# Expert-attention scores: two 128-row products with doubled keys in place of three 64-row products per head

## The reference, cut to what matters

```python
q = _rope(jnp.einsum('bsd,hdp->bhsp', x, Wq))      # P = 64
k = _rope(jnp.einsum('bsd,hdp->bhsp', x, Wk))
v = jnp.einsum('bsd,bhse,hedp->bhsp', x, gv, Wv)
att = jax.nn.softmax(jnp.einsum('bhsp,bhtp->bhst', q, k) / np.sqrt(P), axis=-1)
o = jnp.einsum('bhst,bhtp->bhsp', att, v)
return jnp.einsum('bhsp,bhse,hepd->bsd', o, go, Wo)
```

## Time and profile before

| | |
|---|---|
| median of three runs | 3404.74 us (3403.65 to 3405.85) |
| span of the profiled execution | 3401.4 us |
| time around that span | not listed for that execution; the runs' median is 3.3 us above its span |
| TensorE matmul busy | 3233.1 us, 95% |
| VectorE, ScalarE, GpSimd busy | 2439.7 us (72%), 1961.5 us (58%), 1441.9 us (42%) |
| DMA | 295.18 MB, 32.9% of the 16 engines' span |
| granted TensorE clock | 0.995 of full speed |

### The profile page before, as it was taken

The page is one execution under the profiler, slowest core; times in us unless marked ns, Lnnn a source line. Parts: engine busy times, 40 slices in busy tenths (PEclk is TensorE's granted clock), DMA queues, the critical chain, the costliest instruction groups (busy, mean ns, idle before and its releaser), DMA issues.

```text
span 3401.4 us, 64468 instructions
## 1 busy us (share of the span) xinstructions
PE 3233.1 (95%) x18240; PEld 2378.9 (70%) x18240; DVE 2439.7 (72%) x4708; ACT 1961.5 (58%) x4509; POOL 1441.9 (42%) x1215
## 2 busy tenths in 40 slices
PE   1699999999999999999999999999999999997998
PEld 1577777777777777777777777777777777775765
DVE  6577777777777777777777777777777777775554
ACT  2466666656666666666666666666666666664121
POOL 4144355445443454345543554434534543442212
PEclk9999999999999999999999999999999999999999
DMA  5223333334233333233233332333332433333221
GB/s 165 76 71 87 95 90 85 77 76 109 76 84 87 84 98 81 75 100 96 69 87 76 96 98 77 76 104 81 84 87 68 114 81 75 84 75 110 72 83 62
DMA packets 115937, 295.18 MB, mean 87 GB/s; under 512 B 33856, under 2 KB 54592, under 8 KB 99264
## 3 DMA queue, kind: packets, MB, share of 16 engines
q1 hardware_dynamic: 115904, 294.78, 32.9%
HBM read 262.74 MB, written 31.98 MB: 87 GB/s over the span
## 4 chain that ended last, share of the span: by engine, by line
PE 85%; issue 6%; DVE 5%; ACT 3%; DMA 1%; POOL 0%; ACTq 0%; SPq 0%; DVEq 0%; POOLq 0%
PE bank L673 27%; PE bank L799 22%; PE bank L718 9%; PE bank L773 7%; PE bank L688 5%; PE bank L905 4%; PE bank L897 3%; PE bank L693 3%; PE bank L745 2%; PE bank L754 2%; ACT probs L957 2%; DVE uf L1239 1%; DVE oo L1232 1%; PE bank L694 1%; ACT pt_e L977 1%
## 5 line engine op out<-in xcount | busy, mean ns | idle before, releaser
L573 POOL TENSOR_TENSOR u_l<-uf,u_h 128x512 fp32r<-128x512 f32 x512 | 716.1, 1409 | 722.6 <-ACT u_h L1041 722.4
L1136 DVE TENSOR_REDUCE nmax<-bank 128x1 f32<-128x512 f32 (+3 forms) x1024 | 551.8, 579 | 305.0 <-PE bank L688 297.8
L673 PE MATMUL bank<-wv_h,xx 128*128 128x512 f32 x2048 | 755.0, 410 | 7.1 <-DVE vm L1157 7.1
L957 ACT ACTIVATE probs<-bank,nmax 128x512 f32<-128x512 f32 (+3 forms) x1024 | 590.7, 610 | 253.2 <-DVE nmax L1136 253.1
L1041 ACT ACTIVATE u_h<-uf 128x512 fp32r<-128x512 f32 x512 | 321.7, 632 | 696.9 <-DVE uf L1239 683.6
L673 PEld LDWEIGHTS bank<-wv_h,xx 128*128 128x128 f32 x2048 | 386.0, 188 | 155.8 <-issue 59.6
L718 PEld LDWEIGHTS bank<-ident_sb,probs 128*128 128x128 f32 x3328 | 388.3, 141 | 106.4 <-issue 51.3
L718 PE MATMUL bank<-ident_sb,probs 128*128 128x128 f32 x3328 | 451.3, 274 | 1.6 <-ACT stackT L1032 0.9
L569 POOL TENSOR_TENSOR v_sb<-v_next,zero_hb 128x512 f32<-128x512 f32 x64 | 74.2, 1160 | 891.9 <-PE bank L773 877.4
L799 PE MATMUL bank<-u_h,wo_h 128*128 128x512 f32 x1024 | 427.1, 417 | 5.0 <-ACT u_h L1041 3.2
L1239 DVE TENSOR_TENSOR uf<-oo,go 128x512 f32<-128x512 f32 x512 | 416.2, 823 | 8.8 <-POOL u_l L573 6.6
(11 more groups left out here) (141 smaller groups left out, 5164.2 us busy)
## 6 DMA issues: line engine op xcount, KB each, us to landing
go<-go_d SPq DMA_DIRECT2D x256, 512.0 KB, 6.5
xx<-xs_d SPq DMA_DIRECT2D x128, 512.0 KB, 3.5
oo<-scale_d SPq DMA_DIRECT2D x128, 128.0 KB, 2.9
a_d<-a_out SPq DMA_DIRECT2D x128, 128.0 KB, 2.3
pt_c<-in_x SPq DMA_DIRECT2D x16, 512.0 KB, 4.7
st<-in_wv SPq DMA_DIRECT2D x16, 512.0 KB, 5.8
st<-in_wo SPq DMA_DIRECT2D x16, 512.0 KB, 7.2
go_d<-go_turned SPq DMA_DIRECT2D x256, 8.0 KB
```

The costliest lines, as they stand in the source:

```text
L573: nc.gpsimd.tensor_tensor(u_l[:, e % 2], uf[:, e % 2], u_h.bitcast(f32)[:, e % 2], ALU.subtract).then_inc(ul_done, 1)
L673: last = nc.tensor.matmul(out, lhs, rhs, start=n == 1, stop=n == 3 * len(chunks))
L957: nc.scalar.activation(probs[:, s % 2, j, 0:w], sbank[j][:, 0:w], ACT.Exp, bias=nmax[:, 2 * s + j:2 * s + j + 1], **kw).then_inc(exp_done, 1)
L1136: nc.vector.tensor_reduce(nmax[:, 2 * s + j:2 * s + j + 1], sbank[j][:, 0:w], AX.X, ALU.max, negate=True).then_inc(nmax_ready, 1)
```

## The change

The query's high and low parts of one head are stacked on the 128 partitions: head 0 has its high part on partitions 0 to 63 and its low part on 64 to 127, head 1 the other way round (`q_hl`). The keys' high parts are held twice, on both halves (`k_hh`), and so are the low parts (`k_ll`). One matmul on 128 rows then gives high·high + low·high, a second one high·low + low·low. ScalarE and VectorE write one half each time, so every `QH` and `QL` becomes two instructions on 64 partitions. The second copy of the keys is made by four DMAs from one half of the tile to the other, issued by SyncE in `both_halves`; the scores wait for all four.

```diff
-        q_h = sb("q_h", [NP, S], f32r)
-        q_l = sb("q_l", [NP, S], f32r)
-        k_h = sb("k_h", [NP, S], f32r)
-        k_l = sb("k_l", [NP, S], f32r)
+        q_hl = sb("q_hl", [NP, 2, S], f32r)
+        k_hh = sb("k_hh", [NP, 2, S], f32r)
+        k_ll = sb("k_ll", [NP, 2, S], f32r)
...
+            def both_halves(n):
+
+                for i, (k, made, count) in enumerate(((k_hh, qk_high, 2 * n + 2), (k_ll, k_low, n + 1))):
+                    sp.wait_ge(made, count)
+                    for j in range(2):
+                        here, there = slice(j * P, (j + 1) * P), slice((1 - j) * P, (2 - j) * P)
+                        sp.dma_start(k.bitcast(f32)[there, j, :], k.bitcast(f32)[here, j, :]).then_inc(k_both, 16)
...
                     load_x(after[1], 0)
+                if kind != LAST:
+                    both_halves(it + 1)
                 spread_rden(it)
...
             store_go(0)
+            both_halves(0)
             for half in range(2):
...
-                    for i, (q, k) in enumerate(((q_h, k_h), (q_l, k_h), (q_h, k_l))):
-                        if i > 0:
-                            low_ready(i - 1)
-                        for j in range(2):
-                            rows_j = slice(j * P, (j + 1) * P)
-                            mm = nc.tensor.matmul(sbank[j][:], q[rows_j, qs], k[rows_j, :], start=i == 0, stop=i == 2)
-                            if i == 2:
-                                mm.then_inc(s_full, 1)
+                    for j in range(2):
+                        nc.tensor.matmul(sbank[j][:], q_hl[:, j, qs], k_hh[:, j, :], start=True, stop=False)
+                        nc.tensor.matmul(sbank[j][:], q_hl[:, j, qs], k_ll[:, j, :], start=False, stop=True).then_inc(s_full, 1)
...
-                    pe.wait_ge(qk_high, 2 * n + 2)
-                    scores(0, n, first, low_ready)
+                    at, prior, _ = w_at(kind, it, ("QK", 0))
+                    pe.wait_ge(w_free[at], prior + 1)
+                    pe.wait_ge(k_both, 64 * n + 64)
+                    scores(0, n, first)
...
-                        nc.scalar.activation((q_h, k_h)[i][:], o[:], ACT.Copy, scale=(P ** -0.5, 1.0)[i]).then_inc(qk_high, 1)
+                        for j in range(2):
+                            rows_j = slice(j * P, (j + 1) * P)
+                            last = nc.scalar.activation((q_hl, k_hh)[i][rows_j, j, :], o[rows_j, :], ACT.Copy, scale=(P ** -0.5, 1.0)[i])
+                        last.then_inc(qk_high, 1)
...
-                        if i == 0:
-                            last = nc.vector.scalar_tensor_tensor(q_l[:], o[:], P ** -0.5, q_h.bitcast(f32)[:], ALU.mult, ALU.subtract)
-                        else:
-                            last = nc.vector.tensor_tensor(k_l[:], o[:], k_h.bitcast(f32)[:], ALU.subtract)
+                        for j in range(2):
+                            rows_j, other = slice(j * P, (j + 1) * P), slice((1 - j) * P, (2 - j) * P)
+                            if i == 0:
+                                last = nc.vector.scalar_tensor_tensor(q_hl[other, j, :], o[rows_j, :], P ** -0.5, q_hl.bitcast(f32)[rows_j, j, :], ALU.mult, ALU.subtract)
+                            else:
+                                last = nc.vector.tensor_tensor(k_ll[rows_j, j, :], o[rows_j, :], k_hh.bitcast(f32)[rows_j, j, :], ALU.subtract)
                         last.then_inc(free, 1)
+                        if i == 1:
+                            dve.wait_ge(free, count)
+                            nc.vector.memset(primer[:, 3:4], 0.0).then_inc(k_low, 1)
```

More of the change, by code:

```diff
@@ L219, in build @@
         xn = [rows_view(pc8[:, 4 + 2 * i:6 + 2 * i]) for i in range(2)]
-        x_high = [(q_h[:], k_h[:]), (u_h[:, 0], u_h[:, 1])]
-        x_low = [(q_l[:], k_l[:]), (u_l[:, 0], u_l[:, 1])]
+        x_high = [(q_hl[:, 0], q_hl[:, 1]), (u_h[:, 0], u_h[:, 1])]
+        x_low = [(k_hh[:, 0], k_hh[:, 1]), (u_l[:, 0], u_l[:, 1])]
         level, one, two, odds = (vm[:, i // 2, i % 2 * (S // 2):i % 2 * (S // 2) + TT * NG].rearrange("q (t n) -> q t n", t=TT) for i in range(4))
@@ L280, in build @@
         qk_high = sem("qk_high")
+        k_low = sem("k_low")
+        k_both = sem("k_both")
         rope_ready = sem("rope_ready")
@@ L674, in three, with scores @@
                 return last
-            def scores(s, n, first=False, low_ready=lambda i: None):
+            def scores(s, n, first=False):
                 qt = s // 2
@@ L818, in do, with first_scores @@
                         mix(i)
-                def low_ready(i):
-                    at, prior, _ = w_at(kind, it, ("QK", i))
+                def first_scores(first=False):
+                    at, prior, _ = w_at(kind, it, ("QK", 0))
                     pe.wait_ge(w_free[at], prior + 1)
-                def first_scores(first=False):
-                    pe.wait_ge(qk_high, 2 * n + 2)
-                    scores(0, n, first, low_ready)
+                    pe.wait_ge(k_both, 64 * n + 64)
+                    scores(0, n, first)
                 def stack_turned():
@@ L1214, in do @@
                     elif name == "QL":
-                        o, free, _ = w_filled(("QK", i))
+                        o, free, count = w_filled(("QK", i))
                         dve.wait_ge(qk_high, 2 * n + i + 1)
-                        if i == 0:
-                            last = nc.vector.scalar_tensor_tensor(q_l[:], o[:], P ** -0.5, q_h.bitcast(f32)[:], ALU.mult, ALU.subtract)
-                        else:
-                            last = nc.vector.tensor_tensor(k_l[:], o[:], k_h.bitcast(f32)[:], ALU.subtract)
+                        for j in range(2):
[4 more added lines that the diff above has]
+                                last = nc.vector.tensor_tensor(k_ll[rows_j, j, :], o[rows_j, :], k_hh.bitcast(f32)[rows_j, j, :], ALU.subtract)
                         last.then_inc(free, 1)
+                        if i == 1:
+                            dve.wait_ge(free, count)
+                            nc.vector.memset(primer[:, 3:4], 0.0).then_inc(k_low, 1)
                     elif name == "RECIP":
```

## The result

The changed kernel takes **3521.11 us** (median of four runs, 3520.51 to 3525.64) against 3404.93 us for the kernel before on the same chip: a ratio of 1.0344, with a 95% interval from 1.0329 to 1.0358. It is slower, as forecast, but by 116 us where 53 were forecast, and beyond the end of the range at 3492. TensorE's granted clock is 0.994, against 0.995 before, so the clock has no part in it that could be seen.

A forecast was written before the change was run, and what follows sets the result against it. The chain was taken to lie 85% on TensorE, with SO's delay setting the iteration: 63 × 0.77 = 48.5 us plus 5 for the prologue on 3401.4 gives 3455, plus 3.3 to the median: 3458 us, range 3415 to 3492.

The forecast's parts named there:

- score group: TensorE's score slots: four matmuls, only the first paying change-over, replace three pairs; 0.10 us won per slot.
- halves of `QH` and `QL`: ScalarE and VectorE: each 64-partition instruction costs as much as one of 128, adding 1.20 us to QH0 and QL0.
- `V5` waits for `QL0`: TensorE stands still nearly 1 us for QL0's second half, so V5 starts 0.66 us later than before.
- `SO` starts later by: ScalarE: UH7's 1.62 us delay, partly absorbed by idle time, starts SO 0.92 us late, which turn(7) waits for.
- one iteration longer by, without waits for x: TensorE at turn(7): waiting for SO makes each of 63 iterations 0.77 us longer, 48.5 us in all.
- copies to landing: SyncE's DMA copies of the keys: landing in 2.3 us, hidden by 1 us before TensorE is ready.
- prologue: Before the loop nothing covers the halves, memset, issues and copies' flight: some 5 us once.
- the rival that priced the halves at half: 64-partition instructions cost half, so V5 starts early and iterations win 0.42 us: 3383 us, chance 0.09.
- the change-over: TensorE's time beyond passes in the old score slot, 0.4 of 1.1 us; with the change only the first matmul pays.
- `U7` starts near 10.5 instead of 8.88: VectorE: QL's halves and the memset delay U7, and UH7 on ScalarE by 1.62 us.
- the usual overlap: ScalarE ahead of the last exponentials: 0.1 us added to the idle 0.60, giving 0.70 to absorb delay.
- Behind the four issues on SyncE's queue stands only the denominators' store, which becomes due later than they are issued.: SyncE's DMA queue: the copies' issues hold up nothing; no loss was counted for it.

The follow-up runs named there:

- run 6: The changed kernel with the x load's half 1 issued ahead of the denominators on SyncE, nothing else moved: 3499.98 us, ratio 1.0283.
- run 1: The changed kernel with QH and QL again one 128-partition instruction each (scores of other operands), four copies and four passes kept: 3387.18 us, ratio 0.9954.
- run 2: The kernel before, with only each QH and QL cut into two 64-partition instructions, no copies: 3524.05 us, ratio 1.0354.
- run 10: The changed kernel with U7 before QL0, J6 before V5, x load before denominators, low copies issued per half, SQ right behind UH7: 3385.7 us, ratio 0.9943.
- run 3: The changed kernel with J6 ahead of V5 on TensorE in slot 6: 3520.78 us, ratio 1.0346.
- run 4: The changed kernel with U7 ahead of both QL halves on VectorE: 3473.7 us, ratio 1.0208.
- run 5: The changed kernel with both J6 ahead of V5 and U7 ahead of the QL halves: 3470.29 us, ratio 1.0194.

## Why the prediction was off

| step | forecast | measured |
|---|---|---|
| score group | 0.32, then 0.23 each; next job at its pace | 0.33, then 0.23; `V7` at its pace |
| halves of `QH` and `QL` | full price, 0.59 and 0.69 | 0.59 and 0.69 |
| `V5` waits for `QL0` | about 1 us, 63 times | 0.82 us, 63 times |
| `QL0`'s start to `U7`'s start | 2.6 us | 2.96 us |
| `SO` starts later by | 0.92 us | 1.39 us |
| one iteration longer by, without waits for x | 0.77 us | 1.40 us (run 6, by medians: 1.43) |
| copies to landing | 2.3 us, hidden in the loop | 2.3 us, hidden in the loop |
| prologue | 5 us | the first `SO` to the second 7.6 us longer (38.6 to 46.2), the first iteration in it, 5.4 of it one wait |
| x load | no part in it | 21 us in all (run 6) |

**Right** were the direction, the chain and its places. Four full passes beat three packed pairs, by 0.16 in slot 7 where 0.10 was forecast (3.02 and twice 0.41 are 3.84 and not 3.88, so the forecast had the transposes end 0.04 late): run 1, with the halves' cost taken away, is 15 us faster than before, near the 22 of the rival that priced the halves at half (3383) and so had the same terms left. The Trainium skill's promise of up to 2× for contractions of 64, TensorEngine Tiling (Array Packing), Theoretical Speedup, was rightly set against its own remark on the drain, in Key Properties: the runs agree with the two together, though none shows that the change-over is a drain. The full price of 64 partitions was argued from `SO` and was right, but on thin ground: 1.7 lies between the 1.5 of the data and the 2 of the row's length. Runs 1 and 2 show it by themselves. For VectorE, 689 ns against 692, that agrees with the Trainium skill, VectorE: DVE Perf Modes, Why `tensor_reduce` can't reduce along partition axis, which calls each lane an independent pipeline.

**Mis-sized** was the term "`U7` starts near 10.5 instead of 8.88". It took 0.61 as the pace of VectorE's halves, from `QL0` and `QL1` in a row. The halves came 0.70 apart, their whole duration: with the memset and what lies between the pairs that made 2.96 instead of 2.6. On that chain every tenth counts in full, because ScalarE's spare time was already used up. Of the 0.47 by which `SO` came later than forecast, nearly 0.4 is this. The rest, counted from the iteration's start, is that ScalarE's spare time was 0.6 and not the 0.7 with "the usual overlap", and that slot 3 already came out some 0.07 longer: the gain there was swallowed, as forecast, but `J3` waited 0.18 for `UL3` (11.3 us in 63 iterations), more than the 0.1 won. The other 0.16 stand at `turn(7)`: its second half started 0.13 behind `SO`'s end (1579.30 + 1.94 = 1581.24 to 1581.37) and not 0.05, and, begun anew, took 0.68 to the next job (1581.37 to 1582.05), where in an unbroken `turn(7)` 0.61 are left at that point (run 10: 1514.53 to 1515.57 is 1.04, less the 0.43 after which the forecast has it at its second half). Together 0.63 an iteration, 63 × 0.63 = 40 us. Run 6, whose loop has no wait for x, stands 42 us above the forecast and bears this out.

**Missed** was a wait. The sentence that failed is "Behind the four issues on SyncE's queue stands only the denominators' store, which becomes due later than they are issued." It looked at what the new issues delay, and not at what the delayed `RECIP` holds up on the same queue: the denominators' store and load, and behind those the second half of x, which then also lands later. Its price is 21 us (run 6). The two together, 40 + 21 = 61, are nearly all of the 63 us between 3458 and 3521; the rest is of the size of what the prologue took beyond its 5.

**Confirmed** was also the choice between two waits. The forecast followed the delay of 0.66 at `V5` and that of `SO` apart and let the later one set the iteration. Runs 3 and 4 bear it out: the larger wait in the groups (`V5`, 52 us) was worth nothing alone, the smaller one (`turn(7)`, 17 us) 47.

Not settled is why two halves on VectorE follow each other by their whole duration, where full neighbours overlap by 0.08. No run varied the operation, the partitions or the banks of such a pair by themselves. Nor is it settled why the x load takes longer to land close behind the denominators' load.

## What to carry to other kernels

Here, cutting an instruction of 128 partitions into two of 64 doubled its time on ScalarE and VectorE (0.59 and 0.69 us for each half as for the whole), so a layout that makes TensorE quicker has to be paid for by those engines, and the payment counts where the next engine waits. Where a job is made later, walk down every queue that has something waiting for it, also those of the DMA issues, and ask what unrelated transfer stands behind. When engines wait for each other in a ring, the largest wait is no measure of what its removal wins: several edits here only moved the time to the next wait, and the order that fits the new durations turned 3.4% lost into 0.6% won.

## What was not expected of the hardware

- Pairs of 64-partition instructions on VectorE run 0.70 us apart (1.39 for two), where instructions of 128 partitions on the same data run 0.61 apart, though one alone takes the same 0.69. On ScalarE the halves come 0.60 apart, whole ones 0.57 (`QH0` to `QH1` before).
- The x load, whose data and buffer had been ready for some 1.2 us, cost 16 us of waits in the changed kernel and 42 in run 5. Issued ahead of the denominators it cost none in the loop (run 6).
